# Four places instead of two for the second dense pass of a scan and mixture-of-experts kernel

## The reference

```
it, rt = sigmoid(x @ Wi + bi), sigmoid(x @ Wr + br)
at = exp(-8 * softplus(cap) * rt);  gx = sqrt(1 - at**2) * (it * x)
h  = at * h + gx                                   # scan over the tokens of a sequence
...
scores = sigmoid(x @ gate_w.T);  top 4 of 32 experts by scores + e_bias
combine = scores of the chosen, divided by their sum, zero elsewhere
g, u = x @ w1[e], x @ w3[e]                        # 128 -> 96, for each expert e
out  = sum over e of (silu(g) * u * combine[e]) @ w2[e]
```

## Time and profile before

| | |
|---|---|
| median of three runs | 341.75 us |
| the profiled execution | 343.86 us, of it 342.1 us span (first to last instruction) |
| mean granted TensorE clock | 0.887 of full speed |
| PE busy | 283.5 us (83%) |
| DVE busy | 257.1 us (75%) |
| ACT busy | 217.8 us (64%) |
| first dense pass | about 244 to 292.5 us |
| second dense pass | about 292.5 to 331.2 us |
| end of the last stage | 331.2 to 342.1 us |

### The profile page before, as it was taken

One profiled execution on the slowest core, in us unless ns is written; L12 is line 12 of the kernel. 1 busy time (PEld: TensorE's weight loads), 2 busy tenths in 40 slices (PEclk: granted clock), 3 DMA queues, 4 the chain that ended last, 5 costly groups with the idle time before them and its releaser, 6 DMA issues.

```text
span 342.1 us, 6589 instructions
## 1 busy us (share of the span) xinstructions
PE 283.5 (83%) x1515; PEld 224.0 (65%) x1516; DVE 257.1 (75%) x976; ACT 217.8 (64%) x546; POOL 236.2 (69%) x272
## 2 busy tenths in 40 slices
PE   4575687587674999999998989999999999999760
PEld 2244254454453889889886988888776766898540
DVE  3878679878989477787448978744578887867796
ACT  6938766988683555556554555555588678765672
POOL 4395777777777777777743777777777777777700
PEclk9965666866965699999999999999999999999995
DMA  3999999961111556667646999876511121521222
GB/s 98 313 306 287 280 279 281 307 172 51 47 54 55 155 161 197 185 198 223 200 140 172 250 253 268 236 206 179 148 52 53 47 54 49 141 59 52 67 77 61
DMA packets 83999, 54.81 MB, mean 160 GB/s; under 512 B 8032, under 2 KB 80512, under 8 KB 83968
## 3 DMA queue, kind: packets, MB, share of 16 engines
q1 hardware_dynamic: 57472, 30.85, 33.1%
q0 software_dynamic: 6912, 14.17, 14.5%
q10 hardware_dynamic: 19584, 9.44, 9.8%
HBM read 25.07 MB, written 29.36 MB: 159 GB/s over the span
## 4 chain that ended last, share of the span: by engine, by line
PE 38%; POOL 17%; DVE 13%; ACT 11%; issue 11%; DMA 5%; SPq 4%; POOLq 0%; ACTq 0%; DVEq 0%
POOL xs_dram L404 17%; PE bank L1676 6%; PE bank L1667 6%; PE bank L1672 6%; PE bank L1594 4%; PE bank L1626 3%; SPq L305 3%; DMA xb<-xs_dram 3%; PE bank L1462 3%; PE bank L1495 2%; PE bank L1607 2%; PE bank L1589 2%; PE bank L1455 2%; ACT L460 2%; DVE at_at L1351 1%
## 5 line engine op out<-in xcount | busy, mean ns | idle before, releaser
L413 POOL DMA_INDIRECT yk<-ys_dram,row_ys x108 | 107.4, 994 | 41.5 <-issue 26.8
L404 POOL DMA_INDIRECT xs_dram<-xn_all,row_xs x108 | 108.6, 1006 | 36.2 <-issue 32.3
L1594 PE MATMUL bank<-w,xbT 128*128 x288 | 60.5, 333 | 0.3 <-ACT xbT L617 0.2
L617 ACT COPY xbT<-bank 128x256 f32<-128x256 f32 x72 | 26.8, 373 | 33.1 <-PE bank L1589 29.7
L1092 DVE TENSOR_TENSOR act_a<-silu,bank 128x192 f32<-128x192 f32 x72 | 25.4, 353 | 29.9 <-ACT silu L620 26.2
L1594 PEld LDWEIGHTS bank<-w,xbT 128*128 128x128 f32 x288 | 46.0, 194 | 1.1 <-issue 0.9
L1626 PE MATMUL bank<-w2s,aT 96*128 x288 | 46.0, 282 | 0.1
L1626 PEld LDWEIGHTS bank<-w2s,aT 96*128 96x128 f32 x288 | 37.7, 191 | 2.4 <-issue 1.4
L1676 PE MATMUL bank<-at_at,xn_all 128*128 128x384 f32 (+1 forms) x96 | 34.8, 444 | 4.0 <-DVE at_at L1351 3.9
L1101 DVE COPY yb<-bank 128x256 f32<-128x256 f32 x72 | 30.4, 422 | 8.5 <-PE bank L1626 6.8
L620 ACT ACTIVATE silu<-bank 128x192 f32<-128x192 f32 x72 | 23.8, 331 | 20.1 <-PE bank L1594 19.4
(11 more groups left out here) (216 smaller groups left out, 532.8 us busy)
## 6 DMA issues: line engine op xcount, KB each, us to landing
xb<-xs_dram SPq DMA_DIRECT2D x144, 64.0 KB
ys_dram<-yb ACTq DMA_DIRECT2D x72, 128.0 KB, 2.6
xs_dram<-zeros SPq DMA_DIRECT2D x2, 2048.0 KB, 15.0
ys_dram<-zeros SPq DMA_DIRECT2D x1, 2816.0 KB, 13.4
ys_dram<-zeros SPq DMA_DIRECT2D x1, 2560.0 KB, 18.2
x_sb<-in_L_attn_x_dram SPq DMA_DIRECT2D x8, 256.0 KB, 5.8
xs_dram<-xn_all,row_xs POOLq DMA_INDIRECT x108
yk<-ys_dram,row_ys POOLq DMA_INDIRECT x108, 2.5
```

Source lines behind the costliest of these rows:

```text
L404: pool.indirect_dma_start(out=xs[h], out_offset=bass.IndirectOffsetOnAxis(ap=row_xs[:, j, k:k + 1], axis=0), in_=xn2_all[:, j, :], in_offs ...
L413: pool.indirect_dma_start(out=yk[h][:, j - h * TP, k, :], out_offset=None, in_=ys[h], in_offset=bass.IndirectOffsetOnAxis(ap=row_ys[:, j, ...
L617: act.copy(xbT[:, p, :, :].rearrange("c b t -> c (b t)"), ps_xbT[p][:, 0:2 * P]).then_inc(b_xc[h], 1)
L1594: ins = pe.matmul(ps_gu[o][:, b * 2 * I:(b + 1) * 2 * I].rearrange("t (w a i) -> t w a i", w=2, a=1), xbT[:, o, b, :], w13[:, :, bass.ds(e ...
```

## The change

In the second pass a step has one of four places instead of two. Its gate and up products go to the two halves of one bank (`bank[e % 4]`), which a second pass's width of 256 allows; `silu_e`, `in_e` and `act_e` use both halves of their 512 columns. The Silu of the second pass waits for both products of its step. The gate product of step e waits for `act_e` of step e - 4 instead of e - 2, and the output product is issued three steps behind the gate product instead of one. The shares of the second pass are issued after the products of the third step of three. The first pass is as before, but for PE's order at the seam (steps 25 and 26 have no output product).

```diff
+        DEEP = 4
+        def place(e):
+            if e < PIECES:
+                return e % 2, slice(0, WIDE[0])
+            return e % 2, slice(e % DEEP // 2 * WIDE[1], (e % DEEP // 2 + 1) * WIDE[1])
+        def gates_of(e):
+            if e < PIECES:
+                return ps_dg[e % 2][:, 0:WIDE[0]], ps_du[e % 2][:, 0:WIDE[0]]
+            both = bank[e % DEEP]
+            return both[:, 0:WIDE[1]], both[:, 256:256 + WIDE[1]]
+        def share_place(e):
+            return ps_ds[e // 3 % 2][:, 0:WIDE[e // PIECES]]
+        def free_for(e):
+            return e - 1 if e <= PIECES else max(PIECES, e - DEEP + 1)
...
# ScalarE
-                act.wait_ge(d_gu, 2 * e + 1)
-                ge(act, d_act, e - 1)
-                act.activation(silu_e[e % 2][:, 0:w], ps_dg[e % 2][:, 0:w], ACT.Silu).then_inc(d_silu, 1)
+                i, here = place(e)
+                act.wait_ge(d_gu, 2 * e + 1 + e // PIECES)
+                ge(act, d_act, free_for(e))
+                act.activation(silu_e[i][:, here], gates_of(e)[0], ACT.Silu).then_inc(d_silu, 1)
# VectorE
-                ge(dve, d_y, e - 1)
-                dve.tensor_tensor(act_e[e % 2][:, 0:w], in_e[e % 2][:, 0:w], ps_du[e % 2][:, 0:w], ALU.mult).then_inc(d_act, 1)
+                ge(dve, d_y, free_for(e))
+                dve.tensor_tensor(act_e[i][:, here], in_e[i][:, here], gates_of(e)[1], ALU.mult).then_inc(d_act, 1)
# TensorE
+            def gate_pieces(e):
+                n, q, m = e // PIECES, e % PIECES // 3, e % 3
+                at = slice(q * QUAD * I + m, (q + 1) * QUAD * I, I // PART)
+                ge(pe, d_act, free_for(e))
+                pe.matmul(gates_of(e)[0], w1s[:, at], xd[:, PASS[n]], start=True, stop=True).then_inc(d_gu, 1)
+                if e == 0:
+                    shares_of(0)
+                if m == 1 and e < PIECES:
+                    shares_of(e // 3 + 1)
+                pe.matmul(gates_of(e)[1], w3s[:, at], xd[:, PASS[n]], start=True, stop=True).then_inc(d_gu, 1)
+            def out_piece(e):
+                n, piece = divmod(e, PIECES)
+                i, here = place(e)
+                pe.wait_ge(d_act, e + 1)
+                pe.matmul(ps_out[n], w2p[:, piece, :], act_e[i][:, here],
+                          start=piece == 0, stop=piece == PIECES - 1).then_inc(d_y, 1)
...
-            for e in range(HALVES * PIECES + 1):
-                if e < HALVES * PIECES:
-                    ge(pe, d_act, e - 1)
-                    (gate product, shares, up product)
-                if e:
-                    (output product of e - 1)
+            for e in range(HALVES * PIECES + DEEP - 1):
+                if e < HALVES * PIECES:
+                    gate_pieces(e)
+                if 0 < e <= PIECES:
+                    out_piece(e - 1)
+                if e >= PIECES + DEEP - 1:
+                    out_piece(e - DEEP + 1)
+                if e > PIECES and e % 3 == 2 and e // 3 + 1 < HALVES * E // QUAD:
+                    shares_of(e // 3 + 1)
                 if e == PIECES + 4:
                     turn_back(0)
             turn_back(1)
```

More of the change, by code:

```diff
@@ L85, in sandwich_kernel @@
         PIECES = E * I // P
+        DEEP = 4
+        assert WIDE[1] <= 256
         thirds, third = sb("thirds", [3 * E, D * P], BF16), sb("third", [3 * E, D * P], BF16)
@@ L702, in _ @@
             for e in range(HALVES * PIECES):
-                w = WIDE[e // PIECES]
-                act.wait_ge(d_gu, 2 * e + 1)
-                ge(act, d_act, e - 1)
-                act.activation(silu_e[e % 2][:, 0:w], ps_dg[e % 2][:, 0:w], ACT.Silu).then_inc(d_silu, 1)
+                i, here = place(e)
+                act.wait_ge(d_gu, 2 * e + 1 + e // PIECES)
+                ge(act, d_act, free_for(e))
+                act.activation(silu_e[i][:, here], gates_of(e)[0], ACT.Silu).then_inc(d_silu, 1)
                 between(e)
@@ L1346, in _ @@
                     dve.wait_ge(d_gu, 2)
-                dve.tensor_tensor(in_e[e % 2][:, 0:w], silu_e[e % 2][:, 0:w], ps_ds[e // 3 % 2][:, 0:w], ALU.mult).then_inc(d_in, 1)
+                dve.tensor_tensor(in_e[i][:, here], silu_e[i][:, here], share_place(e), ALU.mult).then_inc(d_in, 1)
                 dve.wait_ge(d_in, e + 1)
                 dve.wait_ge(d_gu, 2 * e + 2)
-                ge(dve, d_y, e - 1)
-                dve.tensor_tensor(act_e[e % 2][:, 0:w], in_e[e % 2][:, 0:w], ps_du[e % 2][:, 0:w], ALU.mult).then_inc(d_act, 1)
+                ge(dve, d_y, free_for(e))
+                dve.tensor_tensor(act_e[i][:, here], in_e[i][:, here], gates_of(e)[1], ALU.mult).then_inc(d_act, 1)
                 between(e)
@@ L1651, in shares_of @@
                 n, q_in = divmod(q, E // QUAD)
-                pe.matmul(ps_ds[q % 2][:, 0:WIDE[n]], owners[:, q_in * QUAD:(q_in + 1) * QUAD, :].rearrange("p e b -> p (e b)"),
+                pe.matmul(share_place(3 * q), owners[:, q_in * QUAD:(q_in + 1) * QUAD, :].rearrange("p e b -> p (e b)"),
                           thirds[:, PASS[n]], start=True, stop=True)
+            def gate_pieces(e):
[10 more added lines that the diff above has]
+                n, piece = divmod(e, PIECES)
+                i, here = place(e)
+                pe.wait_ge(d_act, e + 1)
+                pe.matmul(ps_out[n], w2p[:, piece, :], act_e[i][:, here],
+                          start=piece == 0, stop=piece == PIECES - 1).then_inc(d_y, 1)
             def turn_back(n):
@@ L1660, in turn_back @@
                 ins.then_inc(d_turn, 1)
-            for e in range(HALVES * PIECES + 1):
+            for e in range(HALVES * PIECES + DEEP - 1):
                 if e < HALVES * PIECES:
-                    n, q, m = e // PIECES, e % PIECES // 3, e % 3
-                    at = slice(q * QUAD * I + m, (q + 1) * QUAD * I, I // PART)
-                    ge(pe, d_act, e - 1)
[L1667 to L1672, removed]
-                if e:
[L1674 to L1677, removed]
+                    gate_pieces(e)
[5 more added lines that the diff above has]
+                    shares_of(e // 3 + 1)
                 if e == PIECES + 4:
```

## The result

The changed kernel ran in a median of 341.46 us (19 runs), the kernel before beside it in 342.84 us (19 runs). The ratio is 0.9956, 95% interval 0.9939 to 0.9972: 1.5 us faster, 1.0 to 2.1 by the interval. The forecast was 1.1 us. The three runs of before that the forecast started from (median 341.75) were a little faster than the later ones, so it is the difference that counts.

What follows compares the result with a forecast made beforehand. PE was taken to bound the second pass until the Silu of step 38, then ACT's table loads, then DVE. Gains of 1.55 us less 0.43 give 1.12, so 341.75 - 1.1 = 340.6 us, range 339.4 to 342.2.

Steps and rivals of the forecast that it cites:

- What sets the end: Second pass: PE until the Silu of step 38, then ACT's table loads, then DVE set the kernel's end.
- The terms of the sum: PE queue ahead of step 38: 0.86 + 0.18 + 0.51 = 1.55 us gained, less 0.43 for the Silu's new wait: 1.12.
- the share's 0.18: Share of steps 39 to 41, issued in step 37 before, now follows step 38: 0.18 us less ahead of it.
- the stall's 0.51: PE's stall around the output product of step 35 goes: 0.41 + 0.10 = 0.51 us.
- DVE doesn't hold up PE or ACT before step 38: Second pass: output 34 needs DVE's step 34, done at 307.9; PE asks at 310.4, so PE keeps running.
- The interval of 3.50 us: ACT from Silu 38 to Silu 39, across the table loads: stays 3.50 us, as statistics are there at 313.1.
- the rival by which the load waits for them: ACT's table load waits for the statistics, not the root behind it: 0.4 us gain left, 341.4 us; chance 0.10.
- Nothing gained behind step 39: Steps 39 to 47 and the closing chain are DVE's work and ACT hand-over; all only moves forward by 1.1 us.
- Two products into halves of one bank: Second pass: a second write into one bank waits, 0.16 us a step over steps 25 to 38; 342.9 us; chance 0.06.
- PE's idle time as the gain: All 3.5 us of PE's idle time in the second pass would go: 338.3 us; chance 0.06.
- The clock: PE's granted clock falls in the late second pass; a fall at step 40 gives 343.5 us, behind 44 nothing; chance 0.04.
- The size: Whole kernel 1.1 us faster, 0.3%: 340.6 us against the median of 341.75.

Runs made afterwards that it cites:

- the norms later: Changed kernel with ACT's row normalisations put after steps 41 to 44 instead of 40 to 43; ratio to the kernel before 0.9927, again 0.9942.
- the kernel with the output product one behind: Changed kernel (four places, shared banks, moved shares) with the output product one step behind instead of three; ratio to the kernel before 1.0124.
- the norms in the kernel before: Kernel before with ACT's row normalisations put after steps 41 to 44 instead of 40 to 43; ratio to the kernel before 0.9997.

## Why the prediction was right, point by point

**What sets the end.** Right. PE to the Silu of step 38, ACT's table loads to 39, the hand-over to 41, DVE from there: the two links between ACT and DVE were taken away, one by one and together, and the end moved by 1.53 us for the loads, 1.33 for the hand-over and 2.64 for both. The loads were worth less than DVE's wait of 1.90 behind them, since one of 0.25 came in its place at step 40, with the Silu waiting for PE's product. PE still idled in each, 2.1, 2.1 and 1.3 us from 19.88 us after the mark to its last output product, where it is 2.9 in the changed kernel. DVE's own work, the last link, was not shortened in any experiment.

**The terms of the sum.** 1.55 less 0.43 was forecast, and both parts were measured (17.05 for 18.60 to the gate product of step 38, 1.06 for 0.63 from it to the Silu). Within the 1.55, one output product of 0.43 was measured by itself (18.55 to 18.11). The rest (the other output product's 0.43, the share's 0.18 and the stall's 0.51) is worked out from rows and not measured part by part. The longer wait of the Silu, 0.43 us, cost 2.58 us at the end in the kernel that issues the output product one step behind; three steps behind it counts once.

The Trainium skill (Perfetto Trace Analysis, section Matmuls) wants independent groups of products in different banks. What that would bring here, 0.43 us by the prediction's sum, no run shows: four places with both products in banks of their own would take eight banks, and shares and outputs hold four. Nor was the changed kernel run with a Silu that waits for the gate product alone, so no run shows that the shared bank needs the longer wait.

**DVE doesn't hold up PE or ACT before step 38.** Right. Step 34 started 13.31 us after the mark, 13.22 was worked out. PE was busy for all of the first stretch, and an ACT wait that the profile puts down to DVE's line 1373 (0.9 us, Silu of step 31) ends 0.63 us behind the start of its up product, so it was for PE.

**The interval of 3.50 us.** It stayed, because the statistics came in time: they ran from 312.16 to 312.53, and the first load had been going since 311.68. That also settles the rival by which the load waits for them: it started 0.85 us before their end, where the kernel before had shown 0.15 us.

**Nothing gained behind step 39.** Right: from step 39 to the end it is 25.11 us in the changed kernel and 25.12 in the one before (47.14 - 22.03 and 48.27 - 23.15).

**The other rivals.** Two products into halves of one bank: 0.43 us from gate to up product, as in separate banks, so nothing is paid. PE's idle time as the gain: it would have been 3.5 us, and the list of waits shows it moved rather than gone. The clock: it did fall earlier than before, though not where it hurts. In the changed kernel the turning back took 0.67 us instead of 0.44. In the last 3 us of the pass its clock was 1.00 in the first profile (327.15 to 330.15) and lower in the second, with the same program and the same waits:

```profile
325.80:328.80 3.00, 1.92 (x4) 0.80 (x4) 2.90 (x7) 0.00 (x0) 0.00 (x0) 0.75 0.60 175
```

With the norms later the last two output products took 1.00 and 1.22 us instead of 0.70:

```profile
328.55 1.00 PE L1692 MATMUL bank<-at_at,xn_all 128*128 128x256 f32 x2 [1.22 <-DVE at_at L1373]
329.94 1.22 PE L1692 MATMUL bank<-at_at,xn_all 128*128 128x256 f32 x2 [0.39 <-DVE at_at L1373]
```

From DVE's step 47 to the end it was 12.29 us there, 12.32 in the changed kernel and 12.33 before, so the slack of 1.6 us before DVE takes up the turned output covered it. The prediction's price for a fall behind step 44, nothing, was right; its price for an earlier one was shown in kind, not in size, by the kernel with the output product one behind. One term of that price was too small: it took a product at the lower level for 1.8 times as long, and from start to start it was 0.86 us for 0.43 there, twice as long.

**The size.** The distances give 1.13 us at the end, and the two comparisons 1.5 and 1.1 with intervals that hold it. The 1.8 us of the spans holds 0.67 of scatter ahead of the pass. The absolute forecast of 340.6 us was 0.9 below the 341.46 measured, because it started from three runs of before whose median was 1.1 us under that of all nineteen.

**What failed** was not in the prediction but in two expectations: the 0.7 us of the norms in the kernel before, where I stopped following PE after the step that moved, and the 3 us at most for the output product one step behind, where the clock fell.

## What to carry to other kernels

Deeper buffering paid here through the order in which the producer's queue meets the consumer's answer, not through the places. With the same longer wait of the Silu and the output product one step behind, four places brought Silu 38 only 0.26 us ahead of two; two steps behind already took away all of PE's stalls ahead of it. What a longer lead is worth is read at the next point that doesn't go through that producer, here ACT's table loads: count what no longer stands ahead of the last product that this point needs, and subtract what the new places add to the answer. And once the lead is there, look for hand-overs between the other engines that it now could cover: moving four small blocks of ACT's work by one step gave 1.33 us with the lead and 0.29 without it.

## What was not expected of the hardware

The granted clock of TensorE fell behind a pause of 1.85 us in one kernel and stayed at 1.00 behind 1.77 us in another and 1.50 us in the kernel before. Nor is it fixed by the program: in its two executions the changed kernel had a clock of 1.00 and 0.87 in the 2 us from 34 us after the mark, with PE busy for 0.96 us in both, and its last output product took 0.70 and 1.22 us. The Trainium skill (TensorE: Matmul & The Clock Gate, section A second HAM failure mode: psum-queue depth-cycling) tells of a clock that swings with short pauses between groups; in the pass of the kernel before it did not, and with the output product one step behind it fell and rose once, for a cause that these traces don't show.

A table load took 1.28 us in all traces, and in the changed kernel the root behind it started 0.01 us after its end (311.68 + 1.28 = 312.96, and 312.97). The Trainium skill (ScalarE: Activation LUTs, section What ACT_TABLE_LOAD costs) adds 1.38 us of draining to each switch. Here the first load starts 0.03 us behind the end of the Silu (311.27 + 0.38 = 311.65, and 311.68), so no row leaves room for a drain: a switch and back cost 2 x 1.3 us, and without them DVE's step 39 came 1.85 us earlier. The measured 1.28 decides.
